# Four graph layers on one core: the first batch's order of products, and where the flag for general adjacency is found and read

## What is computed

```python
def _direction(x, W, Wg, b, bg, adj, rel_ids):
    h = x @ W.T
    g = h @ Wg.T
    vals = (h[:, :, None, :] + b) * jax.nn.sigmoid(g[:, :, None, :] + bg)
    onehot = (adj[..., None] == rel_ids).astype(h.dtype)
    return jnp.einsum('bnmr,bmrd->bnd', onehot, vals)
out = _direction(node, W_fwd, Wg_fwd, b_fwd, bg_fwd, adj_mat, rels)          # relations 2 to 40
out = out + _direction(node, W_bwd, Wg_bwd, b_bwd, bg_bwd, adj_t, rels)      # relations 2 to 40
out = out + _direction(node, W_loop, Wg_loop, b_loop, bg_loop, adj_t, rel1)  # relation 1
return jax.nn.relu(out)
```

## Time and profile before

| | |
|---|---|
| three executions | 678.4, 682.18, 681.16 us; median 681.16 |
| the profiled execution | 679.49 us, its span 677.8 us |
| busy in the span | PE 624.0 us (92%), DVE 567.7 (84%), ACT 524.6 (77%), POOL 512.9 (76%) |

### The profile page before, as it was taken

The page is one execution under the profiler, slowest core; times in us unless marked ns, Lnnn a source line. Parts: engine busy times, 40 slices in busy tenths (PEclk is TensorE's granted clock), DMA queues, the critical chain, the costliest instruction groups (busy, mean ns, idle before and its releaser), DMA issues.

```text
span 677.8 us, 17570 instructions
## 1 busy us (share of the span) xinstructions
PE 624.0 (92%) x5965; PEld 457.3 (67%) x5994; DVE 567.7 (84%) x2452; ACT 524.6 (77%) x823; POOL 512.9 (76%) x542
## 2 busy tenths in 40 slices
PE   6999799999779999999999999879999999999984
PEld 4887578777456666666666666657766676676662
DVE  4899769999878888888888889779788888888884
ACT  2654489999778777777777776768998998998984
POOL 2577639999898687777776776668887778887786
PEclk9999999999999999999999999999999999999998
DMA  9910000000000040000000000000000001000011
GB/s 254 287 29 1 2 0 1 2 1 1 0 1 2 2 95 2 2 1 2 1 2 1 2 1 2 3 3 5 18 18 19 18 20 33 19 18 19 19 33 47
DMA packets 35925, 16.79 MB, mean 25 GB/s; under 512 B 8566, under 2 KB 35836, under 8 KB 35836
## 3 DMA queue, kind: packets, MB, share of 16 engines
q1 hardware_dynamic: 32368, 14.46, 8.4%
q10 hardware_dynamic: 3468, 1.20, 0.8%
HBM read 9.59 MB, written 4.19 MB: 20 GB/s over the span
## 4 chain that ended last, share of the span: by engine, by line
PE 65%; DVE 12%; ACT 10%; issue 7%; POOL 4%; ACTq 1%; DMA 1%; DVEq 0%; POOLq 0%
PE pair L1237 20%; PE pair L1451 5%; PE pair L1511 5%; PE quad L1400 4%; ACT arena L971 4%; PE pair L1424 2%; PE pair L1418 2%; PE quad L1294 2%; PE pair L1387 2%; PE quad L1346 2%; PE pair L1371 2%; PE pair L1430 2%; PE quad L1303 2%; PE pair L1303 2%; PE quad L1280 2%
## 5 line engine op out<-in xcount | busy, mean ns | idle before, releaser
L705 POOL TENSOR_TENSOR arena<-arena,nmx 128x1024 f32<-128x1024 f32 x64 | 121.7, 1902 | 57.0 <-DVE nmx L1151 56.8
L1237 PE MATMUL pair<-identf,arena 128*128 128x128 f32 x880 | 121.8, 280 | 0.0
L571 POOL TENSOR_SCALAR X<-yb,ln 128x128 f32<-128x128 f32 x252 | 112.5, 456 | 5.1
L1237 PEld LDWEIGHTS pair<-identf,arena 128*128 128x128 f32 x880 | 94.2, 141 | 25.3 <-issue 24.7
L738 POOL TENSOR_TENSOR arena<-arena,nmx 128x1024 f32<-128x1024 f32 x38 | 72.0, 1896 | 31.3 <-DVE nmx L1125 31.3
L564 POOL TENSOR_TENSOR ln<-ln,neghalf 128x4 f32<-128x4 f32 x63 | 65.9, 1045 | 36.3 <-DVE ln L605 36.2
L918 ACT ACTIVATE arena<-quad 128x1024 f32<-128x1024 f32 x64 | 66.5, 1039 | 25.9 <-PE quad L1354 17.7
L1151 DVE TENSOR_REDUCE nmx<-arena 128x8 f32<-128x1024 f32 x64 | 78.1, 1220 | 1.7
L1142 DVE TENSOR_TENSOR arena<-quad,mask 128x1024 f32<-128x1024 f32 x64 | 77.8, 1215 | 1.7 <-PE quad L1400 1.1
L954 ACT ACTIVATE arena<-arena 128x1024 f32<-128x1024 f32 x64 | 68.2, 1065 | 2.8 <-POOL arena L705 2.8
L1125 DVE CUSTOM_DVE_ANT_0 arena<-quad,arena 128x128 f32<-128x128 f32 x304 | 66.8, 286 | 0.0
(11 more groups left out here) (210 smaller groups left out, 1497.3 us busy)
## 6 DMA issues: line engine op xcount, KB each, us to landing
X<-in_x SPq DMA_DIRECT2D x16, 256.0 KB, 5.5
arena<-in_adj SPq DMA_DIRECT2D x16, 256.0 KB, 6.0
out<-X SPq DMA_DIRECT2D x15, 256.0 KB, 2.4
mask<-sel SPq DMA_DIRECT2D x6, 256.0 KB
mask<-eT SPq DMA_DIRECT2D x48, 6.0 KB
out<-X SPq DMA_DIRECT2D x1, 192.0 KB, 2.1
nat_all<-in_L_gnn_W ACTq DMA_DIRECT2D x2, 64.0 KB, 5.2
w<-in_L_gnn_W ACTq DMA_DIRECT2D x2, 64.0 KB, 5.7
```

The lines of the kernel that those rows point to most:

```text
L571: last = nc.gpsimd.tensor_scalar(x_of(b)[:, cols(g)], y_of(L, b)[:, cols(g)], ln[s][:, g:g + 1], ln[s][:, G + g:G + g + 1], ALU.add, ALU.mult)
L705: nc.gpsimd.tensor_tensor(v3(P2[t % 3], HEADS), v3(P2[t % 3], HEADS), nmx2[t % 2][:].unsqueeze(2).broadcast_to([128, HEADS, N]), ALU.add)\
L1237: last = nc.tensor.transpose(dst[:, cols(i)], src[:, cols(i)], identf[:])
```

## The change

1. `prep_pe` no longer ends with a wait for the last copy. The wait stands now where the matrices are used: before the products of batch 0, before the first product of layer 1, and in the general path.
2. Batch 0 of layer 0 multiplies x by the weights first, for both banks, then waits for the bias and adds it last. The other batches are as before.
3. ACT looks at adj of batch b in its step b up to step 7, and at two batches in each of the steps 8 to 11 (so all 16 are done in step 11). DVE reduces `top` in its step 12 (was 15), PE transposes the column in its step 13 (was after step 15) into bank 7, and DVE sets the flag in its step 14 (was 15).
4. PE reads the flag ahead of the 13 weight matrices (was behind them).
5. DVE sets the ones of the first tile at the start of its step 15 and those of the second after the last statistics of layer 0 (both were at the end of step 15); ACT waits for each where it needs it.

The end of `prep_pe`, and `find_flag`:

```diff
-            pe.wait_ge(sem("prep"), steps[-1] + 1)
...
-            nc.vector.tensor_reduce(toprow[:], bank[0][0:1, 0:128], AX.X, ALU.max).then_inc(sem("top_set"), 1)
+            nc.vector.tensor_reduce(toprow[:], bank[7][0:1, 0:128], AX.X, ALU.max).then_inc(sem("top_set"), 1)
```

ACT, layer 0 and (the last lines) layer 1:

```diff
             def layer0(b, s, turn):
-                if real(b):
-
-                    act.wait_ge(*loaded("adj", b))
-                    need(act, sem("L0_top"), b - 1)
-                    nc.scalar.activation(elu[s][:], adj_of(b), ACT.Relu, bias=minus_one[:],
-                                         accum_out=top[:, bass.ds(b, 1)]).then_inc(sem("L0_top"), 1)
+                half = BATCHES // 2
+                for a in (b,) if b < half else range(2 * b - half, 2 * b - half + 2):
+                    if not real(a):
+                        continue
+                    act.wait_ge(*loaded("adj", a))
+                    need(act, sem("L0_top"), a - 1)
+                    nc.scalar.activation(elu[a % 2][:], adj_of(a), ACT.Relu, bias=minus_one[:],
+                                         accum_out=top[:, bass.ds(a, 1)]).then_inc(sem("L0_top"), 1)
...
-                    if t == 0:
-                        act.wait_ge(sem("ones_row"), 2)
+                    if t < 2:
+                        act.wait_ge(sem("ones_row"), t + 1)
```

DVE, layer 0:

```diff
+            def ones_below(i):
+                dve.wait_ge(sem("L0_hg_mm"), BATCHES - 1 + i)
+                nc.vector.memset(xT[i][96:128, :], 1.0).then_inc(sem("ones_row"), 1)
             def layer0(b, s, turn):
+                if b == BATCHES - 1:
+                    ones_below(0)
...
-                    if b == BATCHES - 1:
+                    if b == BATCHES - 4:
                         dve.wait_ge(sem("L0_top"), BATCHES)
                         nc.vector.tensor_reduce(topmost[:], top[:], AX.X, ALU.max).then_inc(sem("top_set"), 1)
...
-                    if b == BATCHES - 1:
+                    if b == BATCHES - 2:
                         find_flag(dve)
                     stats_dve(dve, 0, b - 1, 1 - s)
-                if b == BATCHES - 1:
-                    dve.wait_ge(sem("L0_hg_mm"), BATCHES)
-                    for i in range(2):
-                        nc.vector.memset(xT[i][96:128, :], 1.0).then_inc(sem("ones_row"), 1)
+                if b == BATCHES:
+                    ones_below(1)
```

PE, layer 0 and (the last lines) layer 1:

```diff
-                    if isinstance(b, int) and b == 0:
+                    if b == 0:
+                        pe.wait_ge(sem("prep"), first)
+                        for g in range(G):
+                            mm(bank[1 + g // 2][:, cols(g % 2, 2 * D)], xT[s][:, cols(g)], hg_w["loop"][:],
+                               start=g % 2 == 0, stop=False)
                         pe.wait_ge(sem("bias_split"), 6)
+                        for i in range(2):
+                            last = mm(bank[1 + i], ones[:], bias3[:], start=False, stop=True)
...
+                    if b == BATCHES - 3:
+                        pe.wait_ge(sem("top_set"), 1)
+                        nc.tensor.transpose(bank[7][0:1, 0:128], topmost[:], identf[:]).then_inc(sem("top_mm"), 1)
                 if b == BATCHES:
-                    pe.wait_ge(sem("top_set"), 1)
-                    nc.tensor.transpose(bank[0][0:1, 0:128], topmost[:], identf[:]).then_inc(sem("top_mm"), 1)
+                    value.append(read_flag(pe))
                     pe.wait_ge(sem("params"), sems["n_params"])
                     pe.wait_ge(sem("pool_ready"), 1)
                     prep_pe(pe, range(first, usual))
-                    value.append(read_flag(pe))
...
+                    if b == 0:
+                        pe.wait_ge(sem("prep"), usual)
                     mm(bank[1], bil[:], xT[s][:], start=True, stop=True).then_inc(sem("L1_u_mm"), 1)
```

More of the change, by code:

```diff
@@ L485, in body @@
                 prep_pe(pe, range(usual, len(prep)))
+                pe.wait_ge(sem("prep"), len(prep))
                 def step(i, g, loop, r):
@@ L1248, in layer0 @@
                     need(pe, sem("L0_vals"), b - 1)
-                    if isinstance(b, int) and b == 0:
-                        pe.wait_ge(sem("bias_split"), 6)
[L1251 to L1255, removed]
+                    if b == 0:
[3 more added lines that the diff above has]
+                               start=g % 2 == 0, stop=False)
+                        pe.wait_ge(sem("bias_split"), 6)
+                        for i in range(2):
+                            last = mm(bank[1 + i], ones[:], bias3[:], start=False, stop=True)
+                    else:
+                        for i in range(2):
+                            mm(bank[1 + 3 * s + i], ones[:], bias3[:], start=True, stop=False)
+                            for g in range(2):
+                                last = mm(bank[1 + 3 * s + i][:, cols(g, 2 * D)], xT[s][:, cols(2 * i + g)], hg_w["loop"][:],
+                                          start=False, stop=g == 1)
                     last.then_inc(sem("L0_hg_mm"), 1)
+                    if b == BATCHES - 3:
+                        pe.wait_ge(sem("top_set"), 1)
+                        nc.tensor.transpose(bank[7][0:1, 0:128], topmost[:], identf[:]).then_inc(sem("top_mm"), 1)
                 if b == BATCHES:
-                    pe.wait_ge(sem("top_set"), 1)
-                    nc.tensor.transpose(bank[0][0:1, 0:128], topmost[:], identf[:]).then_inc(sem("top_mm"), 1)
+                    value.append(read_flag(pe))
                     pe.wait_ge(sem("params"), sems["n_params"])
```

## The result

| | before | changed |
|---|---|---|
| executions, median | 679.35 us (678.4 to 682.18, 6) | 676.26 us (676.01 to 676.45, 6) |
| ratio | | 0.9944, 95% interval 0.9923 to 0.9965 |
| the profiled execution, its span | 679.49, 677.8 us | 676.01, 674.3 us |

By the ratio the changed kernel is faster by 0.56%, about 3.8 us, with an interval from 2.4 to 5.2; the medians lie 3.1 us apart. I had forecast 1.8 us and gave "within 0.5%" the largest chance. The gain is about twice the forecast's. There are also two spreads: the executions of before lie 3.8 us apart, those of the changed kernel 0.4.

What follows compares the result with a forecast made beforehand. Chain through PE or all engines in turns, DVE's pace in layer 0; 0.34 us at the start plus 1.47 at layer 0's end, about 1.8 off 680.3, gave 678.5 us, range 676.0 to 681.2.

Steps and rivals of the forecast that it cites:

- The three places: Where the change touches the wait chain: the start, the middle of layer 0 (DVE's pace), and the end of layer 0.
- if layers 1 to 3 don't simply shift: Sign that the whole prediction is wrong: after layer 0, the later layers were to shift unchanged.
- Part 1: Start: without the wait behind the first three matrices, PE's transposes begin at about 6.71, not 7.05; 0.34 us gained.
- clock rises before batch 0's products: Rival at the start: batch 0's products run at full pace, 2.1 us more gain, 676.4 us; chance 0.10.
- Part 2: Batch 0: bias, complete at 9.83, added last; worth nothing beyond keeping the 0.34, of which the old order loses 0.15.
- Parts 3 and 4: Layer 0's late steps: ACT's double looks cost 0; the earlier flag makes DVE's step 15 begin 0.34 us later.
- Part 6: PE's end of layer 0: flag read taken at 0.98 us; batch 15's aggregation starts 1.82 us earlier, at 72.95.
- Part 7: To layer 1's first exponential: second memset costs DVE's line 0.51; DVE gains 1.31, ACT 1.82, the exponential 1.47 us.
- clock later: Rival at the start: PE's clock rises a batch later, 2.5 to 3.5 us lost, around 681.5 us; chance 0.06.

Runs made afterwards that it cites:

- read_behind: The changed kernel with PE's read of the flag behind the 13 weight matrices again, its wait for the flag still ahead of them; 676.25 us.
- end_only: The changed kernel with its start put back (wait behind the first three matrices, bias first in batch 0); 677.12 us.
- start_only: The kernel before with only the start changed (no wait behind the first three matrices, bias last in batch 0); 679.17 us.
- warm_more: The changed kernel plus 31 unused products in PE's idle stretches at the start; 674.04 us, ratio to before 0.9913.
- warm_fill: warm_more plus 9 and 8 unused products in PE's two idle stretches at the entry of layer 2; 675.10 us.
- bias_first: The changed kernel with the bias first in batch 0, the wait behind the first matrices still gone; 677.18 us.
- before_again: The kernel before, unchanged, run for a second profile; 680.26 us.
- fill_entry: The changed kernel plus 9 unused products on PE at the entry of layer 2, ahead of its wait for layer 1's last rows; 677.21 us.
- ones_old_place: The changed kernel with both memsets of ones back at the end of DVE's step 15; 676.54 us.
- warm_after: The changed kernel plus 22 unused products on PE between the identity and the first weight; 674.95 us.

## Why the prediction was right and wrong

The sum was 0.34 + 1.47 = 1.8 us; the runs show 3.8. Three of its terms failed. The start was mis-sized: 0.34 against 0.9 to 1.1, because the bias was priced at nothing and the pace was held fixed. The end was mis-sized: 1.47 against 2.3, because the read of the flag was priced at its exposed 0.98 and the second memset at 0.51, and both are hidden. And the slower executions of before, worth 0.8 to 1.0 us in the mean, were set aside as scatter: a term put at nothing.

**What bounds the kernel: right.** The three places were the right ones, DVE's pace carried the start's gain through layer 0 unchanged, and layer 1 shifted as it was. Layer 2 didn't: its entry has the new drop of the clock, and my prediction called itself wrong as a whole "if layers 1 to 3 don't simply shift".

**Part 1, the first wait: mechanism right, size wrong.** I had 0.34, the width of the gap in the chain. The transposes start at 6.42 and not at 7.05, 0.63 earlier, because they now also enter PE behind a running product: the chain gives them 0.87 us where they took 1.13 after an idle stretch. With that and without a wait for the bias the products of batch 0 start at 9.17 to 9.33 in the six profiles with the new start (the two with more early work aside), against 9.96 to 10.34 in the five with the old order.

What I left out is the pace. I kept the doubling "just behind the products of batch 0". With the old order it came within the last four products in four profiles and behind them in one, gates at 14.03 to 14.44. With the new order it came within the eight products in three, within the bias products behind them in two and behind these in one (read_behind), gates at 12.40 to 13.54. So it stayed near the end of batch 0's products, as I had it, but these took 3.1 to 4.3 us where they had taken 4.0 to 4.4. In the mean of the profiles the gates moved 1.3 us, 0.8 by the earlier start of the products and 0.5 by the pace; that the second part belongs to the change and isn't the luck of six profiles against five isn't shown. The time moved by 0.86 (end_only against the changed kernel) to 1.1 (start_only's lower group).

Of my rivals "clock rises before batch 0's products" was the nearest and is not what happened. The rule I weighed it by (the Trainium skill, TensorE: Matmul & The Clock Gate, "What's actually happening"), that the instant of the rise isn't tied to the kernel's start, agrees with two profiles of the changed kernel: the products start at 9.33 and 9.29, and the gates come at 12.96 and 12.40. That the rise can be brought forward by earlier work is shown by warm_more and, with the same addition, warm_fill: gates at 10.94 and 10.55, outside the range of the others.

**Part 2, the bias: wrong.** I called it worth nothing beyond 0.15 us. bias_first shows 0.9, all of the start's gain. I took the bias's end from one profile, 9.83, and let it stand. It hangs on a DMA and eight DVE instructions behind it, ended at 9.66 to 10.19 in the profiles without early work, at 10.15 in that of the changed kernel, and PE was ready at 9.33. Even with the old start PE waited for it in three of four profiles (0.27 in before_again).

**Parts 3 and 4, looks and flag: right.** The looks cost nothing. DVE's step 15 became longer as I had it: residual of batch 14 at 57.22 after the gates against 56.30, 0.92 later, forecast 71.51 - 70.74 = 0.77.

**Part 6: the sum's largest term, mis-sized for the wrong reason.** I took the read's 0.98 as exposed because the one row showed it so. It is hidden, at either place (read_behind), though its load takes 0.48 us everywhere. The aggregation of batch 15 comes 2.28 us earlier counted from the gates (60.33 to 58.05), forecast 1.82, and now waits for DVE. My upper bound, "at best 72.3" on the old clock, was what happened: 74.77 - 2.28 = 72.49. What the two removed waits (for ACT's last copy, and for the column of maxima ahead of the matrices) gave, the early read didn't: moving the read ahead of the matrices is worth 0.1 us between gates and exponential, and nothing in the time.

**Part 7: the memset's 0.51 was counted and isn't there.** It lies in the shadow of DVE's read of the flag (0.42 idle after it in place of 1.03). With it, DVE's line gained 2.17 (POOL's subtraction ends at 68.32 after the gates, was 70.49) and not 1.31. ACT's line gained 2.29, so the wait that ends last did not change to DVE's line as I had it: the exponential waits for the table, as before, with POOL 0.06 us ahead of it.

**What no step had: a second kind of execution.** I had the spread of three executions before me, 3.8 us, and treated it as scatter of the measurement. It is a drop of PE's clock to 0.50 behind the idle stretches at the end of layer 0; 32 of 74 executions are in the group that has it, 2.3 us slower in the mean. The change shortens just these stretches, none of the ten profiles with the new end has the drop there, and no execution is in such a group. The account in the runs: 0.9 to 1.1 for the start, 2.3 for the end, 0.2 to 1.3 lost to the new drop at the entry of layer 2 (0.6 in the profile beside the result), and 0.8 (by 2 of the 6 executions measured) to 1.0 (by 32 of 74) for the upper group. That is some 3.4 to 3.8 with the 0.6, and agrees with the measured 3.8 within its interval; it is no closer check than that. My "clock later" case had a drop at the wrong place and with the wrong sign for the change.

**Open.** Why the entry of layer 2 has the drop in both profiles of the changed kernel and in none of the four with the old end of layer 0 isn't settled. Of the ten with the new end seven have it there. The idle stretch is the same, 2.31 us; what has changed is the time at which it comes. Filling it moves the drop to the next one (fill_entry). The two groups of ones_old_place and warm_after differ in their average clock, so a drop of the clock goes with them too; what decides in an execution whether it comes, and how long it lasts, isn't shown. Nor does the average clock always tell the time: in the changed kernel it is anything from 0.989 to 0.996, and the times lie within 0.6 us.

## What to carry to other kernels

Look at the executions one by one before trusting one profile: two groups with little between mean that something switches. Compare the average clock of the executions, and then, in a profile of each group, the granted clock in stretches of 2 us behind PE's idle places. A wait at the end of a helper costs twice, once by itself and once because it exposes whatever stands behind it, such as the load of a register; put the wait where the data are used before moving the load. Where PE must start slow, unused products on data that are there early bring its full pace forward (the gates came 1.5 us earlier here and the time fell by 2.25), but the same filling in the middle of a busy loop can cost what it saves, and can move the drop to the next idle stretch.

## What the runs showed of the hardware that I had not expected

- Idle stretches of PE of 1.2 and 1.3 us with 3.3 us of work between them were followed by nearly 7 us at 1.2 GHz in one profile of the kernel before and not in the other. By times and average clocks 32 of its 74 executions are of the first kind; with 10 unused products in the stretches, none of 12.
- The load of the flag into a register took PE 0.48 to 0.49 us in nine profiles, whether PE stood idle or its products ran. With what stands around it, it shows as 0.98 us where PE had no product left to run, and as a gap of 0.10 us between products in the changed kernel, where it had. DVE's took 0.54 us beside a memset of 0.48.
- The granted clock is shown as 1.00 in the first 13 us, while four records take 1.72 us there and 0.86 later. It shows drops, not the slow start.
- With one idle stretch filled, the drop of the clock came behind the next one, 18 us later, and cost 1.5 us there against 0.6.
